# The first half's residual of a two-layer convolution kernel, moved to ScalarE and an accumulating DMA

## The chip, the core and the metric

The kernel runs on one core of a Trainium2 chip. Its time is the device time of one launch in microseconds (us); a smaller time is better. All numbers below are of this one core. TensorE is called PE in the rows, VectorE DVE, ScalarE ACT, GpSimd POOL, SyncE SP.

## What is computed

The input `x` has 16 images of 128 channels and 64 x 64 pixels. Two residual layers follow each other, each on a group norm of its input (32 groups of 4 channels):

```
def adc(y):                                   # step 2^-8, clip at +-16
    return clip(round(y * 0.01 / step) * step, -16, 16)
# layer 0: quantised input, a cubic term, a 3x3 convolution with three weight planes
v    = dac(_gn(x) * input_factor)             # 8 bits, scaled to 0.6
fv   = patches(v) + 0.1 * patches(v) ** 3
outs = [einsum('bctfyx,ocyx->btfo', fv, g[i]) for i in range(3)]
mem  = adc(outs[2]) + 4 * adc(outs[0]) + 2 * adc(outs[1]) + adc(outs[2])
x    = x + mem * output_factor + bias
# layer 1: q, k, v projections of _gn(x), 64 channels each
out  = q * (eB @ (exp(k) * v)) / (eB @ exp(k))
x    = x + Wm @ out
```

The three `adc` results of layer 0 are whole numbers and are kept as int16; their sum times `fin` (twice the step times the output factor) plus the bias is the layer's output, and it is added to the image.

## The kernel before

One image is a tile `xr[m]` of 128 channels x 4096 pixels in f32; four such tiles form a ring. The work on an image is written as a *phase* of 36 *slots* (0 to 35). Every engine runs its own program, written out slot by slot by `phase`, so the order of each engine is fixed by the tables at the head of the file (`BIAS = (17, 32)`: in slots 17 and 32) and by the order of the `if` lines in `phase`. Engines meet only in semaphores. An instruction that waits holds up all that is behind it on its engine.

In phase p TensorE convolves image p: two halves of 2048 pixels, in each the three planes, which makes six *steps* n = 0 to 5 of six slots each. In every slot TensorE does one product of 9 matmuls (lines 504 to 506) of 512 columns. The rows are transformed beforehand (`transform` on VectorE, `rows_high` on ScalarE, `rows_low` on GpSimd). The products of a step go to a bank pair `A` and to the low pair `B`. `copy_m2` (line 836, ScalarE) copies `B` out, in slot place 2 of each step; `mix_middle` (lines 1192 to 1204, VectorE) forms the four output rows from `A` and the copy; `adc_round` (line 844, ScalarE) turns two of them into int16 in `uall`, and frees the bank pair. It runs two steps late: the rounding of n = 4 stands in slot 0 of the next phase, and TensorE's product in slot 2 of that phase (`middle`, `j == 1`) waits for it. Between these products stands layer 1 of the two images before: in eight slots per phase TensorE does projections (line 586), sums (line 614) and mixes (line 636). Before the projections of slot 32 it waits for `copy_m2` of step 5; before the sums for line 1280 of VectorE.

The end of layer 0 on one half h: `combine_planes` and `first_residual` (VectorE) clip and add the three planes in int16 (lines 1210 to 1225), and line 1228 adds `fin` times the sum to the image. Before that `add_bias` (line 856, ScalarE) has added the bias in place. Then `stats_x1` (line 809, ScalarE, with a one-element shift, line 800, ahead of an image's first) reads the finished pixels in four quarters of 1024, two passes each, for the group norm of layer 1. The first half's quarters stand in slots 26 and 31, the second half's in slots 8 and 9 of the next phase.

Layer 1's output goes back in the way that the change borrows: ScalarE writes it to a buffer `y2` in `shared` (line 901) and GpSimd issues a DMA that adds it to the image (line 1528, 512 KB each, four per image). SyncE loads the image after next (line 404) and stores results (line 414).

A loop of four phases is repeated; the first two phases, phases 2 to 5 and the last three are written out apart.

Of the kernel before, what the change touches and what calls it, by code (L numbers as in the profile page):

```python
# [20 lines left out]
ALU = mybir.AluOpType  # L21
ACT = mybir.ActivationFunctionType
# [44 lines left out]
COMBINE = (20, 0)  # L67
DOUBLE = (17, 35)
RESIDUAL = (23, 8)
BIAS = (17, 32)  # L70
X1_STATS = (26, 31, 8, 9)
X1_SPREAD = 12
X1_GROUP = 15
LOW = (28, 33, 8, 11)
# [28 lines left out]
def conv_layers_kernel(nc, x, g_pos, g_neg, bias, in_factor, out_factor, Wq, Wk, Wv, Bm, Wm, out):  # L103
# [6 lines left out]
    with ctx:  # L110
        def sb(name, shape, dt=F32):
            return ctx.enter_context(nc.sbuf_tensor(name, shape, dt))

        def sem(name):
            return ctx.enter_context(nc.semaphore(name))
# [8 lines left out]
        T = sb("T", [P, 2, 3, H // 4, 2, W], F16)  # L124

        shared = sb("shared", [P, NP * 4 * 3 * P + 4 * 3 * P])
        y2 = [shared[:, k * PX:(k + 1) * PX] for k in range(2)]
        pieces = [shared[:, 4 * PX + k * HALF:4 * PX + (k + 1) * HALF] for k in range(4)]
        t32 = sb("t32", [P, 3, TILES, 2, W])
# [141 lines left out]
        summed = sem("summed")  # L271
        combined = sem("combined")
        biased = sem("biased")
        first_done = sem("first_done")
        tail_part = sem("tail_part")
        tail_stats = sem("tail_stats")
# [443 lines left out]
        def _(act):  # L720
# [94 lines left out]
                channel_stats(0, xr[m], image, q, before)  # L815

            def stats_x1(image, m, q, before):
                act.wait_ge(first_done, nth(image, HALVES, q // 2))
                channel_stats(1, xr[m], image, q, before)

            def last_stats(m):
# [16 lines left out]
            def adc_round(p, n, first):  # L838
                h, i = divmod(n, NP)
                act.wait_ge(conv_ready, nth(p, STEPS, n))  # L840
                if not first or h:

                    act.wait_ge(first_done if i else summed, nth(p, HALVES, h - 1))
                nc.scalar.copy(u[i].rearrange("p (t k c) -> p k t c", k=4, c=W)[:, 0:4:3],  # L844
                               A[n % 2][:, :, :].rearrange("p e (t w) -> p e t w", w=W)).then_inc(rounded, 1)

# [4 lines left out]
                act.wait_ge(inner_made, nth(p, STEPS, NP * h))  # L851
                nc.scalar.activation(u[0], u[0], ACT.Identity, scale=2.0).then_inc(doubled, 1)

            def add_bias(p, m, h):
                xh = xr[m][:, h * HPX:(h + 1) * HPX]
                nc.scalar.activation(xh, xh, ACT.Identity, bias=bcol[:, :]).then_inc(biased, 1)

            def z_high(image, m, k, w):
# [62 lines left out]
            def phase(p, m, images):  # L921
                prev2, prev, cur, nxt = images
                first = not prev
                before, two_before, after = (m + 3) % RING, (m + 2) % RING, (m + 1) % RING
                for slot in range(SLOTS):
                    n, place = divmod(slot, 6)
                    if first and slot == 0:
                        level(0, 0, 3)
                    if first and slot == 1:
                        cubic(0, 3)  # L930
                    if place == 0 and n < 2 and prev and cur:
                        adc_round(p - 1, STEPS - 2 + n, False)
                    if not cur and slot in (0, 2):
                        adc_round(p - 1, STEPS - 2 + slot // 2, False)
                    if place == 0 and n >= 2 and cur:
                        adc_round(p, n - 2, first)
                    if place == 2 and cur:
                        copy_m2(p, n, first)
                    second_layer(p, m, slot, images)
                    if first and slot in (3, 9):  # L940
                        high_weights(1 + slot // 9)
                    if first and slot == 14:
                        small_weights()
                    if nxt and slot in X_STATS:
                        q = X_STATS.index(slot)
                        stats_x(p + 1, after, q, (0, p + 1, q - 1) if q else (1, p - 1, 1) if prev else (0, p, 3))
                    if not cur and slot == X1_STATS[2]:
                        last_stats(before)
                    if prev and cur and slot in X1_STATS[2:]:
                        q = X1_STATS.index(slot)  # L950
                        stats_x1(p - 1, before, q,
                                 (1, p - 1, 2) if q == 3 else (0, p + 1, 3) if nxt else (1, p - 1, 1))
                    if cur and slot in X1_STATS[:2]:
                        q = X1_STATS.index(slot)
                        stats_x1(p, m, q, (1, p, 0) if q else (1, p - 1, 3) if prev else (0, p + 1, 3))
                    if cur and slot in DOUBLE:
                        double(p, DOUBLE.index(slot))
                    if cur and slot in BIAS:
                        add_bias(p, m, BIAS.index(slot))
                    if cur and slot in HIGH[2:]:  # L960
                        rows_high(p, m % 2, HIGH.index(slot))
                    if nxt and slot in LEVEL:
                        level(p + 1, after, LEVEL.index(slot))
                    if nxt and slot in SQUARE:
                        cubic(p + 1, SQUARE.index(slot))
                    if nxt and slot in HIGH[:2]:
                        rows_high(p + 1, 1 - m % 2, HIGH.index(slot))
                if not cur and prev:
                    z_high(p - 1, before, 0, 0)
                    z_high(p - 1, before, 1, 1)  # L970
                    for k in range(NG):
                        exponent(p - 1, k, k)
                        if k < NG - 2:
                            z_high(p - 1, before, k + 2, k + 2)
                        if k:
                            guess(p - 1, k - 1, k - 1)
                    guess(p - 1, NG - 1, NG - 1)
# [22 lines left out]
        def _(dve):  # L1000
# [161 lines left out]
            def mix_middle(p, n, images):  # L1162
# [22 lines left out]
                    dve.wait_ge(t_ready, nth(p, NG, 1))  # L1185
                if i == 0 and (prev or h):
                    dve.wait_ge(summed, nth(p, HALVES, h - 1))
                if i == 1 and (prev or h):
                    dve.wait_ge(first_done, nth(p, HALVES, h - 1))

                near, far = bank[:, 0, :], bank[:, 1, :]
                nc.vector.tensor_tensor(minus, near, m2[:, 0, :], ALU.subtract)  # L1192
# [21 lines left out]
                dve.wait_ge(clipped, nth(p, 2 * HALVES, 2 * h + 1))  # L1214
                nc.vector.tensor_tensor(u[1], u[0], u[1], ALU.add).then_inc(summed, 1)

            def first_residual(p, m, h):

                xh = xr[m][:, h * HPX:(h + 1) * HPX]
                dve.wait_ge(rounded, nth(p, STEPS, NP * h + 2))  # L1220
                dve.wait_ge(inner_made, nth(p, STEPS, NP * h + 2))
                nc.vector.tensor_scalar(u[2], u[2], CLIP, -CLIP, ALU.min, ALU.max).then_inc(clipped_last, 1)
                dve.wait_ge(summed, nth(p, HALVES, h))
                dve.wait_ge(clipped_last, nth(p, HALVES, h))
                nc.vector.tensor_tensor(u[1], u[1], u[2], ALU.add).then_inc(combined, 1)  # L1225
                dve.wait_ge(combined, nth(p, HALVES, h))
                dve.wait_ge(biased, nth(p, HALVES, h))
                nc.vector.scalar_tensor_tensor(out=xh, in0=u[1], scalar=fin[:, :], in1=xh, op0=ALU.mult, op1=ALU.add  # L1228
                                               ).then_inc(first_done, 1)

            def last_residual(m):
# [3 lines left out]
                dve.wait_ge(rounded, nth(p, STEPS, NP * h + 2))  # L1235
                dve.wait_ge(inner_made, nth(p, STEPS, NP * h + 2))
                dve.wait_ge(summed, nth(p, HALVES, h))
                dve.wait_ge(biased, nth(p, HALVES, h))
                for c in range(2):
                    cols = slice(c * PX, (c + 1) * PX)  # L1240
                    xh = xr[m][:, (2 + c) * PX:(3 + c) * PX]
# [15 lines left out]
            def last_sums(m):  # L1257


                count = 1.0 * PX  # L1260
                dve.wait_ge(first_done, HALVES * B)
                for h in range(2):
                    at = 3 * PX + h * HALF
                    nc.vector.bn_stats(hst[:, h, :], xr[m][:, at:at + HALF]).then_inc(tail_stats, 1)
# [80 lines left out]
            def phase(p, m, images):  # L1345
# [3 lines left out]
                for slot in range(SLOTS):  # L1349
# [17 lines left out]
                        g = TRANSFORM.index(slot)  # L1367
                        transform(p, g, mixed(p, slot))
                    if prev and cur and slot == RESIDUAL[1]:
                        first_residual(p - 1, before, 1)  # L1370
                    if not cur and slot == 3:
                        last_residual(before)
                        last_sums(before)
# [8 lines left out]
                    if cur and slot == COMBINE[0]:  # L1382
                        combine_planes(p, 0)
                    if cur and slot == RESIDUAL[0]:
                        first_residual(p, m, 0)
                    if nxt and slot in QUANTISE:
                        quantise(p + 1, QUANTISE.index(slot))
                    if nxt and slot in CUBIC:
# [45 lines left out]
        def _(pool):  # L1434
# [90 lines left out]
            def add_mix(image, m, k):  # L1525
# [2 lines left out]
                nc.gpsimd.dma_start(xr[m][:, k * PX:(k + 1) * PX], y2[k % 2], accum_op=ALU.add  # L1528
                                    ).then_inc(y_added[k % 2], 16)

            def second_layer(p, m, slot, images):

                at = second("Z_POOL", p, slot, images)
                if at:
                    z_rest(at[0], at[2])
                at = second("ADD_POOL", p, slot, images)
                if at:
                    add_mix(at[0], (m + at[1]) % RING, at[2])

            def phase(p, m, images):  # L1540
                prev2, prev, cur, nxt = images
                before, two_before = (m + 3) % RING, (m + 2) % RING
                for slot in range(SLOTS):
                    second_layer(p, m, slot, images)
                    if cur and slot in LOW[2:]:
                        rows_low(p, m % 2, LOW.index(slot))
                    if nxt and slot in LOW[:2]:
                        rows_low(p + 1, 1 - m % 2, LOW.index(slot))
                    if nxt and slot == X_MOMENTS:
                        scale_x(p + 1)  # L1550
                    if prev and slot == X1_MOMENTS:
                        scale_z(p - 1)
# [37 lines left out]
```

## Time and profile before

| | |
|---|---|
| time, median of 3 runs | 1532.73 us (1531.08 to 1533.22) |
| profiled execution, span from first to last instruction | 1530.4 us |
| TensorE busy | 1446.2 us, 95% |
| VectorE busy | 1402.8 us, 92% |
| ScalarE busy | 1191.8 us, 78% |
| GpSimd busy | 521.5 us, 34% |
| mean granted TensorE clock | 0.984 |
| DMA | 103.91 MB, 68 GB/s mean |

Of the profiled execution only the span is given; the median of the runs is 2.3 us above it. The middle of the program is periodic: between two neighbouring images the same instructions come 89.2 us later, so one period can be read for all. A matmul's record lasts about 0.38 us, but the next starts 0.216 us after it; the busy time of TensorE counts overlaps once. A row of the timeline gives start, duration, engine, line, operation, output and input, and in brackets how long the engine was idle before and who ended it.

### The profile page before, as it was taken

To read this page: it belongs to the slowest core of one execution; us is meant where nothing else is said; L and a number is where in the kernel's file an instruction comes from. 1 tells how busy PE (TensorE), PEld (TensorE's weight loads), DVE (VectorE), ACT (ScalarE), POOL (GpSimd) and SP (SyncE) were. 2 spreads that over 40 slices of the span, in tenths; PEclk is the share of its full clock that TensorE was granted. 3 is DMA by queue.
4 is the path that set the end of the run, shared out by engine and by line. 5 is a ranking of instruction groups with operands and counts; after the bars stand their busy time and mean duration, and the time that the engine had idled before them with its cause. 6 is when DMAs were issued, how large, how long until landed. Compare 5 with 4: busy or idle time off the path is not lost.

```text
span 1530.4 us, 24432 instructions
## 1 busy us (share of the span) xinstructions
PE 1446.2 (95%) x8560; PEld 645.4 (42%) x8560; DVE 1402.8 (92%) x2185; ACT 1191.8 (78%) x1561; POOL 521.5 (34%) x503
## 2 busy tenths in 40 slices
PE   2799999999999999999999999999999999999975
PEld 2444444444444444444444444444444444444422
DVE  7879999999999999999999998999999999999766
ACT  4557788788878878887887888788788878876563
POOL 3111334234333433333343343334333333433312
PEclk9799999999999999999999999999999999999997
DMA  5011012223122222312222231232223122212222
GB/s 208 1 56 42 14 28 56 83 56 111 42 64 89 56 83 56 111 42 69 84 56 84 56 111 43 57 96 56 83 56 110 39 62 95 56 28 56 69 70 83
DMA packets 29180, 103.91 MB, mean 68 GB/s; under 512 B 4032, under 2 KB 4224, under 8 KB 29056
## 3 DMA queue, kind: packets, MB, share of 16 engines
q1 hardware_dynamic: 20416, 70.86, 12.4%
q0 software_dynamic: 8640, 31.46, 10.9%
q8 instruction: 70, 1.15, 0.3%
q14 instruction: 54, 0.44, 0.1%
HBM read 37.29 MB, written 33.55 MB: 46 GB/s over the span
## 4 chain that ended last, share of the span: by engine, by line
DVE 50%; PE 28%; issue 14%; ACT 5%; POOL 1%; DVEq 1%; DMA 0%; SPq 0%; ACTq 0%; POOLq 0%
PE A L504 5%; PE A L505 5%; PE A L506 5%; DVE duo L1132 3%; DVE uall L1225 3%; DVE A L1195 3%; DVE A L1204 3%; DVE uall L1198 3%; DVE duo L1192 3%; DVE uall L1200 2%; DVE duo L1193 2%; DVE A L1196 2%; DVE f L1109 2%; PE B L504 2%; PE B L505 2%
## 5 line engine op out<-in xcount | busy, mean ns | idle before, releaser
L504 PE MATMUL A<-T,WH 128*128 128x504 f16 (+1 forms) x1152 | 438.4, 381 | 0.0
L506 PE MATMUL A<-T,WL 128*128 128x504 f16 (+1 forms) x1152 | 437.3, 380 | 0.0
L505 PE MATMUL A<-T,WH 128*128 128x504 f16 (+1 forms) x1152 | 437.3, 380 | 0.0
L1521 POOL TENSOR_TENSOR T<-t,T 128x512 f16<-128x512 f32 x189 | 254.9, 1374 | 424.8 <-ACT T L766 424.8
L1495 POOL TENSOR_TENSOR zl<-z,zh 128x512 f16<-128x512 f32 x120 | 158.5, 1337 | 434.3 <-ACT zh L877 434.3
L809 ACT ACTIVATE junk<-xr,shift 128x1024 f16<-128x1024 f32 x244 | 280.1, 1148 | 5.5
L504 PE MATMUL B<-T,WH 128*128 128x504 f16 (+1 forms) x576 | 221.0, 384 | 19.1 <-DVE T L1158 11.5
L505 PE MATMUL B<-T,WH 128*128 128x504 f16 (+1 forms) x576 | 220.9, 383 | 0.0
L506 PE MATMUL B<-T,WL 128*128 128x504 f16 (+1 forms) x576 | 220.7, 383 | 0.0
L504 PEld LDWEIGHTS A<-T,WH 128*128 128x128 f16 x1152 | 115.4, 100 | 164.3 <-issue 46.4
L506 PEld LDWEIGHTS A<-T,WL 128*128 128x128 f16 x1152 | 112.7, 98 | 136.2
L505 PEld LDWEIGHTS A<-T,WH 128*128 128x128 f16 x1152 | 112.7, 98 | 117.9
L746 ACT ACTIVATE q<-xr,bi,sc 128x1024 int16<-128x1024 f32 x64 | 79.2, 1240 | 62.6 <-DVE f L1109 40.9
L844 ACT CAST uall<-A 128x1024 int16<-128x1024 f32 x96 | 96.2, 1002 | 32.3 <-PE A L506 32.0
L836 ACT COPY m<-B 128x1024 f32<-128x1024 f32 x96 | 96.0, 1000 | 30.0 <-PE B L506 30.0
L766 ACT CAST T<-t 128x512 f16<-128x512 f32 x192 | 105.7, 614 | 9.9 <-DVE t L1148 9.6
L504 PEld LDWEIGHTS B<-T,WH 128*128 128x128 f16 x576 | 56.6, 98 | 100.7 <-issue 21.8
L881 ACT ACTIVATE shared<-L 128x512 f32<-128x512 f32 x61 | 36.2, 593 | 66.6 <-PE L L586 66.6
L1228 DVE SCALAR_TENSOR_TENSOR xr<-uall,fin,xr 128x2048 f32<-128x2048 int16 x31 | 85.9, 2770 | 1.1
L506 PEld LDWEIGHTS B<-T,WL 128*128 128x128 f16 x576 | 56.8, 99 | 69.7 <-issue 2.8
L901 ACT ACTIVATE shared<-B 128x1024 f32<-128x1024 f32 x60 | 61.3, 1022 | 31.9 <-PE B L636 31.9
L1528 POOL DMA_DIRECT2D xr<-shared x60 | 53.3, 889 | 92.4 <-ACT shared L901 92.4
(186 smaller groups left out, 2563.7 us busy)
## 6 DMA issues: line engine op xcount, KB each, us to landing
xr<-in_x_dram SPq DMA_DIRECT2D x64, 512.0 KB, 5.8
out_dram<-xr SPq DMA_DIRECT2D x64, 512.0 KB, 2.7
xr<-shared POOLq DMA_DIRECT2D x60, 512.0 KB, 4.5
xr<-in_L_conv_g_pos_dram SPq DMA_DIRECT2D x3, 576.0 KB, 9.8
xr<-in_L_conv_g_neg_dram SPq DMA_DIRECT2D x3, 576.0 KB, 11.6
xr<-in_L_conv_Wm_dram SPq DMA_DIRECT2D x2, 32.0 KB, 9.6
xr<-in_L_conv_Wq_dram SPq DMA_DIRECT2D x1, 32.0 KB, 11.6
xr<-in_L_conv_Wk_dram SPq DMA_DIRECT2D x1, 32.0 KB, 11.4
```

What stands on the lines that cost most here:

```text
L504: nc.tensor.matmul(to, wh, th, start=fresh and y == 1, stop=False, skip_group_check=True)
L505: nc.tensor.matmul(to, wh, tl, start=False, stop=False, skip_group_check=True)
L506: done = nc.tensor.matmul(to, wl, th, start=False, stop=y == 2, skip_group_check=True)
L746: nc.scalar.activation(q16[b][:, :], xr[m][:, q * PX:(q + 1) * PX], ACT.Identity, bias=bi1[:, :], scale=sc1[:, :]).then_inc(leveled, 1)
L766: nc.scalar.copy(T[:, 0, pair, g * TILES:(g + 1) * TILES, :, :], t32[:, pair]).then_inc(th_ready, 1)
L809: nc.scalar.activation(junk[:, :], src[:, q * PX:(q + 1) * PX], func, bias=shift[which][:, :], accum_out=moments[which][:, k, q:q + 1]).th ...
L836: nc.scalar.copy(m2[:, :, :], low_pair[:, :, :]).then_inc(m2_copied, 1)
L844: nc.scalar.copy(u[i].rearrange("p (t k c) -> p k t c", k=4, c=W)[:, 0:4:3], A[n % 2][:, :, :].rearrange("p e (t w) -> p e t w", w=W)).the ...
L901: nc.scalar.activation(y2[k % 2].rearrange("p (r c n) -> p c r n", r=2, n=QUART), low_pair[:, :, :].rearrange("p c (r n) -> p c r n", r=2) ...
L1228: nc.vector.scalar_tensor_tensor(out=xh, in0=u[1], scalar=fin[:, :], in1=xh, op0=ALU.mult, op1=ALU.add).then_inc(first_done, 1)
L1495: nc.gpsimd.tensor_tensor(zl[0][:, cols], z32[:, cols], zh[0][:, cols], ALU.subtract).then_inc(zl_ready, 1)
L1521: last = nc.gpsimd.tensor_tensor(low, t32[:, pair, :, :, :].rearrange("p t e w -> p (t e w)"), high, ALU.subtract)
```

## The change

For the first half of an image (h = 0) line 1228 and its `add_bias` go. In their place a new `first_output` on ScalarE computes `fin * sum + bias` from the int16 sum into `y1`, 2048 columns of `shared` that are free by then, and a new `first_add` on GpSimd issues one DMA of 1 MB that adds `y1` to the first half of the image. The statistics of the first two quarters wait for that DMA and stand in slots 31 and 34 in place of 26 and 31. The second half is as before.

```
-BIAS = (17, 32)
-X1_STATS = (26, 31, 8, 9)
+OUTPUT = 26
+OUTPUT_ADD = 27
+BIAS = 32
+X1_STATS = (31, 34, 8, 9)
...
+        y1 = shared[:, 2 * PX:4 * PX]
...
             def stats_x1(image, m, q, before):
-                act.wait_ge(first_done, nth(image, HALVES, q // 2))
+                if q < 2:
+                    act.wait_ge(first_added, nth(image, 16, 15))
+                else:
+                    act.wait_ge(first_done, nth(image, 1, 0))
                 channel_stats(1, xr[m], image, q, before)
...
+            def first_output(p):
+                act.wait_ge(combined, nth(p, HALVES, 0))
+                if isinstance(p, int) and p == 0:
+                    act.wait_ge(small_done, 1)
+                    act.wait_ge(w_turned, 9)
+                else:
+                    act.wait_ge(first_added, nth(p, 16, 15, 1))
+                nc.scalar.activation(y1, u[1], ACT.Identity, bias=bcol[:, :], scale=fin[:, :]).then_inc(y1_made, 1)
...
-            def add_bias(p, m, h):
-                xh = xr[m][:, h * HPX:(h + 1) * HPX]
+            def add_bias(p, m):
+                xh = xr[m][:, HPX:2 * HPX]
...
-            def first_residual(p, m, h):
+            def sum_planes(p, h):
...
                 nc.vector.tensor_tensor(u[1], u[1], u[2], ALU.add).then_inc(combined, 1)
-                dve.wait_ge(combined, nth(p, HALVES, h))
-                dve.wait_ge(biased, nth(p, HALVES, h))
+
+            def first_residual(p, m):
+                xh = xr[m][:, HPX:2 * HPX]
+                dve.wait_ge(combined, nth(p, HALVES, 1))
+                dve.wait_ge(biased, nth(p, 1, 0))
                 nc.vector.scalar_tensor_tensor(out=xh, in0=u[1], scalar=fin[:, :], in1=xh, op0=ALU.mult, op1=ALU.add
                                                ).then_inc(first_done, 1)
...
                     if cur and slot == RESIDUAL[0]:
-                        first_residual(p, m, 0)
+                        sum_planes(p, 0)
...
+            def first_add(p, m):
+                waits_apart(pool, (y1_made, nth(p, 1, 0)))
+                nc.gpsimd.dma_start(xr[m][:, 0:HPX], y1, accum_op=ALU.add).then_inc(first_added, 16)
```

The waits that guard `u[1]` and `u[2]` (in `adc_round` and `mix_middle`) are put on the new semaphores: plane 1 of the second half waits for `y1_made`, plane 2 for `combined`.

ScalarE in slots 26 to 32 of a phase in the middle, before (`m` is the copy of the low pair, `xr,shift` the statistics, `uall<-A` the rounding, `T<-t` the rows, `f<-q` the square of the quantised input):

```order
L836 COPY m<-B 128x1024
L800 ACTIVATE shift<-xr 128x1
L809 ACTIVATE junk,moments<-xr,shift 128x1024 x2
L756 ACTIVATE f<-q 128x1024
L844 CAST uall<-A 128x2x8x64
L766 CAST T<-t 128x512 x3
L809 ACTIVATE junk,moments<-xr,shift 128x1024 x2
L836 COPY m<-B 128x1024
```

The same slots now:

```order
L844 COPY m<-B 128x1024
L878 ACTIVATE shared<-uall,bcol,fin 128x2048
L761 ACTIVATE f<-q 128x1024
L859 CAST uall<-A 128x2x8x64
L771 CAST T<-t 128x512 x3
L805 ACTIVATE shift<-xr 128x1
L814 ACTIVATE junk,moments<-xr,shift 128x1024 x2
L844 COPY m<-B 128x1024
```

The new output pass has taken the place of the first quarter's statistics, and these, with their shift, now stand behind the rows and right ahead of the copy of step 5.

ScalarE from slot 32 to slot 0 of the next phase, before (`shared<-L` and `shared<-B` are exponents, logarithm and query copy of layer 1, `z` and `zh` its normalised input, `uall<-uall` the doubling):

```order
L856 ACTIVATE xr<-xr,bcol 128x2048
L766 CAST T<-t 128x512 x3
L887 ACTIVATE shared<-L 128x512
L889 ACTIVATE shared<-shared 128x512
L893 COPY shared<-B 128x512
L872 ACTIVATE z<-xr,bi,rs 128x1024
L877 CAST zh<-z 128x1024
L852 ACTIVATE uall<-uall 128x2048
L844 CAST uall<-A 128x2x8x64
```

The same stretch now:

```order
L882 ACTIVATE xr<-xr,bcol 128x2048
L771 CAST T<-t 128x512 x3
L913 ACTIVATE shared<-L 128x512
L915 ACTIVATE shared<-shared 128x512
L919 COPY shared<-B 128x512
L814 ACTIVATE junk,moments<-xr,shift 128x1024 x2
L898 ACTIVATE z<-xr,bi,rs 128x1024
L903 CAST zh<-z 128x1024
L867 ACTIVATE uall<-uall 128x2048
L859 CAST uall<-A 128x2x8x64
```

The second quarter's statistics have come in ahead of `z`, and so ahead of the rounding of step 4, the last row.

GpSimd from slot 18 to slot 35, before (`zl` is the low part of layer 1's input, `T` the low part of the rows, six pieces in two groups):

```order
L1495 TENSOR_TENSOR zl<-z,zh 128x512 x2
L1528 DMA xr<-shared 128x1024
L1495 TENSOR_TENSOR zl<-z,zh 128x512 x2
L1521 TENSOR_TENSOR T<-t,T 128x512 x6
L1495 TENSOR_TENSOR zl<-z,zh 128x512 x2
L1528 DMA xr<-shared 128x1024
```

The same slots now:

```order
L1529 TENSOR_TENSOR zl<-z,zh 128x512 x2
L1562 DMA xr<-shared 128x1024
L1529 TENSOR_TENSOR zl<-z,zh 128x512 x2
L1569 DMA xr<-shared 128x2048
L1555 TENSOR_TENSOR T<-t,T 128x512 x6
L1529 TENSOR_TENSOR zl<-z,zh 128x512 x2
L1562 DMA xr<-shared 128x1024
```

The new DMA, twice as wide as the others, is issued ahead of the low parts of the rows; nothing else has moved.

## Rows read from the trace of the kernel before

**Rows 1.** Page, part 1: busy us, share of the span, instructions.
```profile
PE 1446.2 (95%) x8560; PEld 645.4 (42%) x8560; DVE 1402.8 (92%) x2185; ACT 1191.8 (78%) x1561; POOL 521.5 (34%) x503
```
**Rows 2.** Stretch 700 to 800: length, busy PE, PEld, DVE, ACT, POOL, clock, DMA share, GB/s.
```profile
700.00:800.00 100.00, 99.28 (x583) 44.11 (x582) 95.17 (x158) 84.00 (x108) 38.99 (x42) 1.00 0.26 72
```
**Rows 3.** Waits of PE, whole run: us in total, times, longest.
```profile
PE L L614 <- DVE shared L1280: 8.3, 15, 0.9
...
PE L L586 <- ACT m L836: 4.2, 12, 0.7
```
**Rows 4.** Page, part 4: the chain that ended last, by engine.
```profile
DVE 50%; PE 28%; issue 14%; ACT 5%; POOL 1%; DVEq 1%; DMA 0%; SPq 0%; ACTq 0%; POOLq 0%
```
**Rows 5.** Timeline of PE, slot 32 to slot 2 of the next phase.
```profile
741.64 1.05 PE L586 MATMUL L<-zh,wqkv 128*64 128x512 f16 x8 [0.21 <-ACT m L836]
...
747.47 1.09 PE L614 MATMUL L<-shared,eb 64*64 64x256 f32 x16 [0.51 <-DVE shared L1280]
...
756.29 0.38 PE L504 MATMUL A<-T,WH 128*128 128x512 f16 x1
```
**Rows 6.** Timeline of ACT, slot 24 to slot 0 of the next phase.
```profile
725.54 1.24 ACT L746 ACTIVATE q<-xr,bi,sc 128x1024 int16<-128x1024 f32 x1 [0.63 <-DVE f L1109]
...
729.85 1.01 ACT L836 COPY m<-B 128x1024 f32<-128x1024 f32 x1
730.75 0.20 ACT L800 ACTIVATE shift<-xr 128x1 f32<-128x1 f32 x1
730.99 1.15 ACT L809 ACTIVATE junk<-xr,shift 128x1024 f16<-128x1024 f32 x1
...
735.63 1.01 ACT L844 CAST uall<-A 128x1024 int16<-128x1024 f32 x1 [1.18 <-PE A L506]
...
738.18 1.15 ACT L809 ACTIVATE junk<-xr,shift 128x1024 f16<-128x1024 f32 x1
...
740.59 0.99 ACT L836 COPY m<-B 128x1024 f32<-128x1024 f32 x1
...
745.22 1.99 ACT L856 ACTIVATE xr<-xr,bcol 128x2048 f32<-128x2048 f32 x1
...
750.29 1.24 ACT L872 ACTIVATE z<-xr,bi,rs 128x1024 f32<-128x1024 f32 x1
...
752.52 1.91 ACT L852 ACTIVATE uall<-uall 128x2048 int16<-128x2048 int16 x1
754.33 0.99 ACT L844 CAST uall<-A 128x1024 int16<-128x1024 f32 x1
```
**Rows 7.** Line 1228 in the whole run: min, median, max in ns.
```profile
L1228 DVE SCALAR_TENSOR_TENSOR xr<-uall,fin,xr x31: 2351/2352/3308, 114.7 to 1444.9; 128x2048 f32<-128x2048 int16 x31
```
**Rows 8.** Timeline of DVE: the sum of the first half's planes, and line 1280.
```profile
726.21 1.23 DVE L1225 TENSOR_TENSOR uall<-uall 128x2048 int16<-128x2048 int16 x1
...
746.64 0.69 DVE L1280 SCALAR_TENSOR_TENSOR shared<-L,shared 128x512 f32<-128x512 f32 x1
```
**Rows 9.** Timeline: an ACT pass into the buffer, and the DMA issue that waits for it.
```profile
718.38 1.01 ACT L901 ACTIVATE shared<-B 128x1024 f32<-128x1024 f32 x1
```
**Rows 10.** The same place on POOL.
```profile
719.94 0.96 POOL L1528 DMA_DIRECT2D xr<-shared  x1 [4.64 <-ACT shared L901]
```
**Rows 11.** Line 1528 in the whole run: from issue to landing.
```profile
DMA to landing us min/median/max: 4.5/4.5/6.1
```
**Rows 12.** Page, part 3, the queue of line 1528: packets, MB, share of 16 engines.
```profile
q0 software_dynamic: 8640, 31.46, 10.9%
```
**Rows 13.** Timeline of PE, a pause in the first phases.
```profile
135.81 0.38 PE L504 MATMUL B<-T,WH 128*128 128x512 f16 x1 [2.30 <-issue]
```
**Rows 14.** Stretch 135 to 140, columns as in rows 2.
```profile
135.00:140.00 5.00, 4.19 (x13) 1.68 (x14) 4.90 (x8) 3.33 (x6) 0.71 (x1) 0.70 0.10 16
```
**Rows 15.** Timeline of ACT and PE in the last image's phases.
```profile
1471.35 1.24 ACT L872 ACTIVATE z<-xr,bi,rs 128x1024 f32<-128x1024 f32 x1
...
1474.48 1.41 PE L586 MATMUL L<-zh,wqkv 128*64 128x512 f16 x8 [2.79 <-DVE shared L1296]
```

More of the change, by code:

```diff
@@ L273, in conv_layers_kernel @@
         biased = sem("biased")
+        y1_made = sem("y1_made")
+        first_added = sem("first_added")
         first_done = sem("first_done")
@@ L841, in adc_round @@
                 if not first or h:
-                    act.wait_ge(first_done if i else summed, nth(p, HALVES, h - 1))
+                    if i == 0:
+                        act.wait_ge(summed, nth(p, HALVES, h - 1))
+                    elif i == 2:
+                        act.wait_ge(combined, nth(p, HALVES, h - 1))
+                    elif h:
+                        act.wait_ge(y1_made, nth(p, 1, 0))
+                    else:
+                        act.wait_ge(first_done, nth(p, 1, 0, 1))
                 nc.scalar.copy(u[i].rearrange("p (t k c) -> p k t c", k=4, c=W)[:, 0:4:3],
@@ L852, in double @@
                 nc.scalar.activation(u[0], u[0], ACT.Identity, scale=2.0).then_inc(doubled, 1)
-            def add_bias(p, m, h):
-                xh = xr[m][:, h * HPX:(h + 1) * HPX]
+            def first_output(p):
[3 more added lines that the diff above has]
+                    act.wait_ge(w_turned, 9)
+                else:
+                    act.wait_ge(first_added, nth(p, 16, 15, 1))
+                nc.scalar.activation(y1, u[1], ACT.Identity, bias=bcol[:, :], scale=fin[:, :]).then_inc(y1_made, 1)
+            def add_bias(p, m):
+                xh = xr[m][:, HPX:2 * HPX]
                 nc.scalar.activation(xh, xh, ACT.Identity, bias=bcol[:, :]).then_inc(biased, 1)
@@ L957, in phase @@
                         double(p, DOUBLE.index(slot))
-                    if cur and slot in BIAS:
-                        add_bias(p, m, BIAS.index(slot))
+                    if cur and slot == OUTPUT:
+                        first_output(p)
+                    if cur and slot == BIAS:
+                        add_bias(p, m)
                     if cur and slot in HIGH[2:]:
@@ L1187, in mix_middle @@
                     dve.wait_ge(summed, nth(p, HALVES, h - 1))
-                if i == 1 and (prev or h):
-                    dve.wait_ge(first_done, nth(p, HALVES, h - 1))
+                if i == 1 and h:
+                    dve.wait_ge(y1_made, nth(p, 1, 0))
+                elif i == 1 and prev:
+                    dve.wait_ge(first_done, nth(p, 1, 0, 1))
                 near, far = bank[:, 0, :], bank[:, 1, :]
@@ L1215, in combine_planes @@
                 nc.vector.tensor_tensor(u[1], u[0], u[1], ALU.add).then_inc(summed, 1)
-            def first_residual(p, m, h):
-                xh = xr[m][:, h * HPX:(h + 1) * HPX]
+            def sum_planes(p, h):
                 dve.wait_ge(rounded, nth(p, STEPS, NP * h + 2))
@@ L1237, in last_residual @@
                 dve.wait_ge(summed, nth(p, HALVES, h))
-                dve.wait_ge(biased, nth(p, HALVES, h))
+                dve.wait_ge(biased, nth(p, 1, 0))
                 for c in range(2):
@@ L1260, in last_sums @@
                 count = 1.0 * PX
-                dve.wait_ge(first_done, HALVES * B)
+                dve.wait_ge(first_done, B)
                 for h in range(2):
@@ L1369, in phase @@
                     if prev and cur and slot == RESIDUAL[1]:
-                        first_residual(p - 1, before, 1)
+                        sum_planes(p - 1, 1)
+                        first_residual(p - 1, before)
                     if not cur and slot == 3:
@@ L1546, in phase @@
                         rows_low(p, m % 2, LOW.index(slot))
+                    if cur and slot == OUTPUT_ADD:
+                        first_add(p, m)
                     if nxt and slot in LOW[:2]:
```

## The prediction, made before the changed kernel was run

> **What bounds the kernel now.** The page's chain of waits puts half of the span on VectorE [rows 4], and VectorE is busy 92% [rows 1]. That reads as if each VectorE instruction taken away were time won. So the next view is the busy time in a stretch of the middle: from 700 to 800 us TensorE is busy 99.28 of 100, VectorE 95.17, ScalarE 84.00 [rows 2]. TensorE is the wall; the chain only runs over VectorE because the two are close. The list of waits then says what is left to win: TensorE waits for VectorE's line 1280 before the sums, 8.3 us in the whole run, and for ScalarE's copy of the low pair before the projections, 4.2 us [rows 3], 12.5 us together. Both stand in one place of the period, slots 32 and 33: 0.21 us at 741.64 and 0.51 at 747.47 [rows 5].
>
> Last the timeline of ScalarE around that place, since the change puts its work there. ScalarE waits for TensorE at 735.63; from then on it is behind. Its copy of step 5 starts at 740.59 and is what TensorE waits for at 741.64; the rounding of step 4 runs from 754.33 to 755.3 [rows 6], and TensorE's product that needs it starts at 756.29 without a wait [rows 5]. So there is 0.96 us of room at the second place and none at the first.
>
> **What is removed.** Line 1228 on the first half, 16 of its instructions. The fastest of them takes 2.35 us [rows 7], so at least 38 us of VectorE's busy time go. The whole of it lies beside TensorE's work. It can pay no more than TensorE's waits for VectorE, 8.3 us, since line 1280 at 746.64 [rows 8] comes about 2 us sooner. I take that 0.5 us per image as won, inside the sum below. `add_bias` on the first half (1.99 us, as in rows 6) goes from slot 17, where ScalarE next waits for GpSimd: worth nothing.
>
> **What is added on ScalarE.** The output pass reads 2048 int16 per partition. Nearest rows: the doubling, int16, 1.91 us; the bias pass, 1.99; and a pass with scale and bias both from memory takes 1.24 for 1024 columns [rows 6] against 1.01 for one without [rows 9], so 0.2 more. I take 2.1 us; bounds 1.9 and 2.5 (twice 1.24). It stands behind the copy of step 4, which ends near 730.8 [rows 6]. The sum it needs ends at 727.44 [rows 8], so it does not wait. The level pass at 725.54 waited 0.63 us for VectorE [rows 6], and a less burdened VectorE gives most of that back, so I start the output pass at 730.2 and end it at 732.3. ScalarE had idle time there, 1.18 us before 735.63 plus what the first quarter's statistics (730.75 to 733.4) leave: covered.
>
> **The DMA.** GpSimd's issue starts 0.55 us after the pass (718.38 + 1.01 = 719.39 to 719.94) [rows 9, 10]. From issue to landing the 512 KB DMAs of this kind take 4.5 us [rows 11]. Their queue's packets take 10.9% of the span [rows 12], 166.8 us over 60 DMAs, 2.78 us each. So 1.7 us are fixed, and 1 MB should take 1.7 + 5.6 = 7.3 us. Landing: 732.3 + 0.55 + 7.3 = 740.15. The bounds are 4.5 us (size costs nothing) and 9.0 (twice all of it), so 737.35 to 742.2 with the passes' bounds.
>
> The Trainium skill, "DMA: Bandwidth & Descriptors", section "Anatomy of one DMA — SWDGE (gpsimd) path", fits a DMA issued by GpSimd with about 2.0 us plus bytes at 436 GB/s. By that 512 KB would take 3.2 us and the new one 4.4 (an estimate from the page). This trace does not agree for the accumulating kind: it shows 4.5 at 512 KB [rows 11].
>
> **First wait, slot 31.** Behind the rows, ScalarE is free at 738.18 [rows 6] and now waits for the landing until 740.15, 2.0 us. Then come the shift, 0.24 (730.75 to 730.99), and the quarter's two passes, 2.41 (738.18 to 740.59). The copy of step 5 starts at 742.8 in place of 740.59: 2.2 us late. Queued behind it are the projections of slot 32, on TensorE itself, so TensorE stands 2.4 us there in place of 0.2. At the sums the old 0.5 us goes. Net after that point: 1.7.
>
> **Second wait, slot 0.** ScalarE's exponent, output copy and bias pass follow TensorE's projections and are late by the same 2.2 us. Then, ahead of `z` (750.29), the second quarter's 2.41 us are new. The rounding of step 4 ends at 755.33 + 2.2 + 2.4 = 759.9, and TensorE's product of slot 2 starts then, not at 756.29. That is 3.6 us late per image, whatever was lost at the first wait: 2.2 + 2.4 less the room of 0.96. Behind it ScalarE has idle places and VectorE is no longer full, so both are level with TensorE again by the middle of the next phase. The loss comes back once per image.
>
> In the rows, it adds to 14 images, the phases 1 to 14: 14 x 3.6 = 50. In phase 0 layer 1 is missing and ScalarE has room: I put 1 there, a choice. In the last phases ScalarE's `z` at 1471.35 would come 2.4 + 0.5 us later, and TensorE's projections at 1474.48 hang on it [rows 15]: 3. Sum 54, on a span of 1530.4: 1584.4. The median of the runs lies 2.3 above the profiled span, so **1587 us**.
>
> Bounds: if the DMA lands before ScalarE asks (4.5 us), only 0.24 + 2.41 - 0.96 = 1.7 per image stays, 24 + 3, which gives 1560. If it takes 9.0 us, landing at 742.2, the loss is 4.3 + 2.4 - 0.96 = 5.7 per image, 80 + 5, which gives 1618.
>
> **The rivals.**
> 1. *The DMA is hidden, only the order costs.* As the lower bound: 1560 (1553 to 1569). For it: the fixed part may cover more than the 1.7 us. Against it: 2.78 of the present DMA's 4.5 us are packets [rows 11, 12]. The Trainium skill's fit named above would give this case, 4.4 us against the 5.3 that are free between the issue at 732.85 and 738.18.
> 2. *The clock falls on top.* After a pause of 2.30 us in front of 135.81 [rows 13] the granted clock is 0.70 over the next 5 us, and TensorE's work there is 13 matmuls against 5 / 0.216 = 23 at full pace [rows 14]. The level granted in part of that stretch is the lower one, 1.2 GHz. My first wait is 2.4 us long, as much as that one. If each brings 1.5 us (half of a 3 us stretch at the low level), 14 x 1.5 = 21: 1608 (1600 to 1625). Against it: part of that is spent before ScalarE's late rounding anyway.
> 3. *Faster, since VectorE is the bound.* The place is slots 32 and 33: with VectorE 2.35 us ahead, TensorE's waits there fall away, at most 12.5 us over the run, which gives 1520 (1518 to 1529). It decides if ScalarE's new work at 738 to 755 costs less than the 0.96 us of room plus its idle time, so if the landing comes before 738 and the 2.4 us of the second quarter find gaps. For it: rows 4. Against it: ScalarE has no bracket of idle time in front of 738.18, 740.59, 750.29, 752.52 or 754.33 [rows 6]; it is full there.
> 4. *No change*: the gains of 3 and the losses meet, or the wait sits where nobody is late: 1533.
>
> **How the numbers follow.** The forecast (landing after 738.18, both waits) gets 0.60, with 1570 to 1600 as its own range. Rival 1 gets 0.13, rival 2 0.14, rival 3 0.08, rival 4 0.05. The range reaches from rival 1 to the upper bound and into rival 2: 1556 to 1618. About 0.2% (3 us) is what a measurement of this kernel can tell from no change. Slower: forecast and rivals 1 and 2, 0.87; within it: 0.05; faster: 0.08.
>
> **What the profile after would show.** Right: line 814's first pass behind the rows is preceded by about 2 us of ScalarE idle, ended by the DMA of line 1569; that DMA takes near 7.3 us from issue to landing; the projections of slot 32 show TensorE idle about 2.4 us, released by the copy of the low pair; the product of slot 2 shows about 2 us, released by the rounding; the sums of slot 33 show no wait for VectorE; the period is 92.8 us in place of 89.2. VectorE's busy time falls by about 40 us. Wrong in size: landing at 4.5 us or at 9. Wrong in kind: the period is 89 or less, which would mean that ScalarE's work of slots 30 to 36 has more room than the timeline shows; or the granted clock is below 1.00 in the middle, which is rival 2.

## The result, and the profile after

The changed kernel takes 1608.45 us (1602.46 to 1610.01, 4 runs) against 1531.9 before: a ratio of 1.049, 95% interval 1.047 to 1.051. It is slower, as forecast, and inside the range; the point of 1587 us was 21 us too low.

The page of the kernel after, busy time and the chain that ended last:

```profile
PE 1466.0 (91%) x8560; PEld 648.1 (40%) x8560; DVE 1400.4 (87%) x2169; ACT 1191.1 (74%) x1561; POOL 547.0 (34%) x519
...
DVE 30%; PE 24%; ACT 19%; issue 16%; DMA 7%; POOL 3%; DVEq 0%; ACTq 0%; SPq 0%; POOLq 0%
```

Against [rows 1] VectorE's and ScalarE's busy times are nearly the same in a longer span, TensorE's is 20 us longer over the same 8560 instructions, and GpSimd's is 25.5 us longer over 16 more. Against [rows 4] ScalarE's share of the chain has risen from 5% to 19% and the DMA's from 0% to 7%. TensorE's waits say where:

```profile
PE L L591 <- ACT m L844: 43.1, 15, 3.6
PE A L509 <- ACT uall L859: 24.5, 14, 1.9
```

The first is the wait for the copy of step 5, 4.2 us in [rows 3]; the second, for the rounding of step 4, was not there. Both come once per image. Periods are counted from TensorE's group statistics in slot 14, which stand at 828.4 here and at 701.5 in the kernel before. ScalarE in the period from 828.4 on, the answer to [rows 6]:

```profile
852.56 1.24 ACT L751 ACTIVATE q<-xr,bi,sc 128x1024 int16<-128x1024 f32 x1 [0.70 <-DVE f L1137]
...
857.77 2.10 ACT L878 ACTIVATE shared<-uall,bcol,fin 128x2048 f32<-128x2048 int16 x1
...
862.58 1.01 ACT L859 CAST uall<-A 128x1024 int16<-128x1024 f32 x1 [1.76 <-PE A L511]
863.49 1.66 ACT L771 CAST T<-t 128x512 f16<-128x512 f32 x3
867.46 0.20 ACT L805 ACTIVATE shift<-xr 128x1 f32<-128x1 f32 x1 [2.31 <-DMA xr<-shared]
...
870.11 0.99 ACT L844 COPY m<-B 128x1024 f32<-128x1024 f32 x1
...
879.80 1.15 ACT L814 ACTIVATE junk<-xr,shift 128x1024 f16<-128x1024 f32 x1
...
882.22 1.23 ACT L898 ACTIVATE z<-xr,bi,rs 128x1024 f32<-128x1024 f32 x1
...
886.25 0.99 ACT L859 CAST uall<-A 128x1024 int16<-128x1024 f32 x1
```

The output pass runs from 857.77 to 859.87. ScalarE is done with the rows at 865.15 and stands still until the DMA has landed, 2.31 us. From 867.46 it has no pause of its own until 870.11. The second quarter (879.80) stands ahead of `z`, and the rounding ends at 887.24. The DMA itself, line 1569, all 16:

```profile
DMA to landing us min/median/max: 6.9/7.0/8.3
```

TensorE in the same period, the answer to [rows 5]: 2.78 us at the projections, no wait at the sums, 1.90 at slot 2.

```profile
871.16 1.05 PE L591 MATMUL L<-zh,wqkv 128*64 128x512 f16 x8 [2.78 <-ACT m L844]
...
876.41 1.10 PE L619 MATMUL L<-shared,eb 64*64 64x256 f32 x16
...
887.29 0.39 PE L509 MATMUL A<-T,WH 128*128 128x512 f16 x1 [1.90 <-ACT uall L859]
```

Two neighbouring periods of the kernel after, columns as in [rows 2]:

```profile
734.20:828.40 94.20, 90.10 (x529) 39.15 (x529) 85.38 (x133) 74.62 (x99) 34.31 (x33) 0.98 0.30 79
828.40:921.60 93.20, 88.52 (x529) 38.71 (x529) 85.43 (x133) 74.66 (x99) 34.36 (x33) 1.00 0.30 80
```

The undisturbed period is 93.2 us, 4.0 more than the 89.2 of before. The other has 1.0 on top and a mean clock of 0.98. Its cause stands behind the first wait; TensorE's row, and the windows of the stretch:

```profile
776.96 1.05 PE L591 MATMUL L<-zh,wqkv 128*64 128x512 f16 x8 [2.77 <-ACT m L844]
```
```profile
776.00:778.20 2.20, 1.25 (x12) 0.60 (x12) 2.20 (x5) 0.90 (x2) 0.00 (x0) 1.00 0.00 0
778.20:781.60 3.40, 3.40 (x23) 1.23 (x20) 2.65 (x5) 1.57 (x3) 0.00 (x0) 0.50 0.00 0
```

After a pause of 2.77 us the granted clock is 0.50, the lower level of 1.2 GHz, for 3.4 us. Such a fall came in 11 of the 14 periods, and in none of the 14 of before.

So the 77.5 us that the span grew by (1530.4 to 1607.9) are: 14 x 4.05 = 57 of waits at full clock; 15 put down to the clock, as a difference (the 14 periods sum to 1323.5 us; 14 x 93.2, and the 3.8 us by which the 14 before exceed 14 x 89.14, make 1308.6; 11 falls of 3.4 us at half the clock could cost at most 19); 6 after the last period (118.0 against 111.9 us); less 0.3 in the stretch ahead of the first period.

### The profile page after: what moved, and what is told of

The parts are those of the page before. It is cut to its first block, busy times and chain, and to the rows that moved or that the text cites. A ratio compares the mean times of both kernels' runs of the same rounds, so it can differ in the third digit from the quotient of the medians.

```text
span 1607.9 us, 24442 instructions
## 1 busy us (share of the span) xinstructions
PE 1466.0 (91%) x8560; PEld 648.1 (40%) x8560; DVE 1400.4 (87%) x2169; ACT 1191.1 (74%) x1561; POOL 547.0 (34%) x519
## 4 chain that ended last, share of the span: by engine, by line
DVE 30%; PE 24%; ACT 19%; issue 16%; DMA 7%; POOL 3%; DVEq 0%; ACTq 0%; SPq 0%; POOLq 0%
DMA xr<-shared 7%; PE A L509 4%; PE A L510 4%; PE A L511 4%; PE L L591 4%; ACT z L898 3%; PE B L641 3%; ACT junk L814 3%; POOL zl L1529 3%; DVE f L1137 2%; DVE A L1225 2%; DVE A L1234 2%; DVE uall L1228 2%; DVE duo L1222 2%; ACT uall L859 2%
## 5 line engine op out<-in xcount | busy, mean ns | idle before, releaser
L1555 POOL TENSOR_TENSOR T<-t,T 128x512 f16<-128x512 f32 x189 | 244.8, 1320 | 431.3 <-ACT T L771 431.3
L1529 POOL TENSOR_TENSOR zl<-z,zh 128x512 f16<-128x512 f32 x120 | 176.7, 1489 | 454.8 <-ACT zh L903 454.8
L591 PE MATMUL L<-zh,wqkv 128*64 128x512 f16 x492 | 71.3, 415 | 51.7 <-ACT m L844 43.1
L1160 DVE TENSOR_TENSOR duo<-f 128x1024 f32<-128x1024 f32 x64 | 91.6, 1432 | 7.6 <-POOL T L1555 3.7
L1562 POOL DMA_DIRECT2D xr<-shared x60 | 58.7, 978 | 94.8 <-ACT shared L927 89.5
L1222 DVE TENSOR_TENSOR duo<-A,m 128x512 f32<-128x512 f32 x96 | 65.6, 683 | 26.8 <-issue 17.7
```

What stands on the lines that cost most here:

```text
L591: last = nc.tensor.matmul(out, lhsT, src, start=m == 0, stop=m == 2, skip_group_check=True)
L1160: nc.vector.tensor_tensor(flat, f[:, at + 2:at + 2 + ROWS, :], f[:, at:at + ROWS, :], ALU.subtract).then_inc(delta_made, 1)
L1529: nc.gpsimd.tensor_tensor(zl[0][:, cols], z32[:, cols], zh[0][:, cols], ALU.subtract).then_inc(zl_ready, 1)
L1555: last = nc.gpsimd.tensor_tensor(low, t32[:, pair, :, :, :].rearrange("p t e w -> p (t e w)"), high, ALU.subtract)
```

## The experiments

Each is timed against the kernel before, run again on the same chip; its medians there were 1531.9, 1532.2 and 1532.0 us, so the runs can be compared with each other too.

**Order alone.** Kernel before, without the new DMA and the output pass:
```
-X1_STATS = (26, 31, 8, 9)
+X1_STATS = (31, 34, 8, 9)
```


> The kernel before with one table changed: the first half's statistics in slots 31 and 34 in place of 26 and 31. VectorE's residual, the bias pass and all DMAs stay. Theory (ScalarE is full from slot 30 to slot 0 of the next phase, with 0.96 us of room): the shift (0.24) and one quarter (2.41) more stand ahead of the rounding of step 4, so TensorE's product of slot 2 waits 1.7 us per image; 14 images and about 3 at the end give 1532 + 27 = 1559 us, and TensorE's wait at the projections of slot 32 grows by only 0.24. Rival (the loss is the DMA's alone, its wait and its traffic): no change, 1532 us.

Measured: 1558.77 us, ratio 1.017 (1.016 to 1.019). TensorE's waits:
```profile
PE A L504 <- ACT uall L844: 20.5, 14, 1.6
...
PE L L586 <- ACT m L836: 8.1, 15, 0.7
```
The wait at slot 2 is there without the new DMA. 27 us of the loss are the place of the statistics.

**The DMA's landing.** Kernel after:
```
-        first_added = sem("first_added")
+        first_added = [sem("first_added0"), sem("first_added1")]
...
-                    act.wait_ge(first_added, nth(image, 16, 15))
+                    act.wait_ge(first_added[q], nth(image, 16, 15))
...
-                nc.gpsimd.dma_start(xr[m][:, 0:HPX], y1, accum_op=ALU.add).then_inc(first_added, 16)
+                for c in range(2):
+                    cols = slice(c * PX, (c + 1) * PX)
+                    nc.gpsimd.dma_start(xr[m][:, cols], y1[:, cols], accum_op=ALU.add).then_inc(first_added[c], 16)
```


> The changed kernel with its 1 MB DMA issued as two of 512 KB, each with its own semaphore, so that a quarter's statistics wait only for their own part. Theory (the first loss is ScalarE's wait for the landing): the first lands 4.5 us after its issue, when ScalarE is just free; ScalarE's 2.3 us of waiting and most of TensorE's 2.8 us at slot 32 go, the granted clock no longer falls, and the 1.7 to 2.1 us at slot 2 stay: 1560 to 1566 us. Rival (the traffic of the added 1 MB, or GpSimd's issue of it, is what costs): two issues cost at least as much as one, 1600 us or more.

Measured: 1556.53 us, ratio 1.016 (1.014 to 1.017), the same as with the order alone and some 4 us under the theory's range.
```profile
PE A L509 <- ACT uall L859: 26.3, 14, 2.1
...
PE L L591 <- ACT m L844: 8.6, 15, 1.6
```
The wait for the copy fell from 43.1 to 8.6 us, and the clock's falls from 11 of 14 periods to 1. The 1 MB still moves. So 52 us, the falls of the clock included, hung on when the first quarter lands.

**The traffic.** Kernel before, with one more DMA per image that nobody waits for:
```
...
+                nc.gpsimd.dma_start(shared[:, 3 * PX:4 * PX], shared[:, 2 * PX:3 * PX], accum_op=ALU.add
+                                    ).then_inc(extra, 16)
...
```


> The kernel before with one more accumulating DMA of 512 KB per image, inside a free part of the shared buffer, issued by GpSimd in slot 27 as in the changed kernel, which nobody but the next one of its kind waits for. Theory (the traffic and its issue cost nothing by themselves): 1532 us within 0.2%. Rival (the added traffic slows engines or the other DMAs): half of the unexplained part, 1540 us or more.

Measured: 1532.75 us, ratio 0.9997 (0.999 to 1.001). An added DMA of 512 KB and its issue cost nothing that can be measured here. That is half of the change's bytes.

**VectorE's part alone.** Kernel before:
```
-                nc.vector.scalar_tensor_tensor(out=xh, in0=u[1], scalar=fin[:, :], in1=xh, op0=ALU.mult, op1=ALU.add
-                                               ).then_inc(first_done, 1)
+                n = HPX if h else 1
+                nc.vector.scalar_tensor_tensor(out=xh[:, 0:n], in0=u[1][:, 0:n], scalar=fin[:, :], in1=xh[:, 0:n],
+                                               op0=ALU.mult, op1=ALU.add).then_inc(first_done, 1)
```


> The kernel before with VectorE's residual of an image's first half over 1 of its 2048 columns (the other 2047 are left without the first layer's output), so that some 36 us of VectorE's work are gone and nothing is put in their place. Theory (TensorE bounds, VectorE is only close): TensorE's wait for line 1280 at slot 33, 0.5 us per image, goes and nothing else: 1525 us, down to 1520. Rival (VectorE bounds, as the chain of waits reads): 1532 - 36 = 1496 us.

Measured: 1526.08 us, ratio 0.996 (0.994 to 0.998). This is all that freeing VectorE brings by itself. By the theory TensorE's wait for it at the sums would be gone; it fell from 8.3 to 4.8 us:
```profile
PE L L614 <- DVE shared L1281: 4.8, 14, 0.6
```
VectorE's busy time fell by 10.4 us only, though the shortened instruction gave up 34. In 14 of its 64 places the next `duo<-f` takes 2.17 us in place of 1.22, each time beside GpSimd's `zl`:
```profile
817.15 2.45 POOL L1496 TENSOR_TENSOR zl<-z,zh 128x512 f16<-128x512 f32 x2 [9.19 <-ACT zh L877]
```
```profile
818.51 2.17 DVE L1132 TENSOR_TENSOR duo<-f 128x1024 f32<-128x1024 f32 x1
```

**The bias pass in slot 17.** Kernel after, `BIAS = 32` to `BIAS = 17`:

> The changed kernel with the second half's bias pass in slot 17, where ScalarE waits for GpSimd, in place of slot 32. Theory (slot 2's wait is ScalarE being full between slots 30 and 0): 1.99 us leave that stretch, the 2.0 us wait of slot 2 goes, the 2.8 us at slot 32 and the falls of the clock stay: 1608 - 14 x 2.0 = 1580 us. Rival (the second wait only follows from the first, as everything behind a late DMA): 1605 us or more, since the first is untouched.

Measured: 1597.04 us, ratio 1.043 (1.041 to 1.045). Neither number came. The wait at slot 2 went from 2.06 us (the 1.90 of the row and what the pipeline hides) to 1.46. ScalarE shows why:
```profile
871.78 0.60 ACT L913 ACTIVATE shared<-L 128x512 f32<-128x512 f32 x1 [1.20 <-PE L L619]
```
Of the 1.99 us taken out, 1.20 are now idle time in front of the logarithm, which waits for TensorE's sums. What counts at slot 2 is the row of work behind the sums, and the bias pass stands ahead of it. The clock fell in 5 periods only, though the pauses ahead were as long as before (2.7 to 4.1 us, against 2.7 to 3.7). The two profiled executions are 15.8 us apart: 14 x 0.57 = 8 us are the undisturbed period, 92.6 in place of 93.2, some 6 are the clock, by the same difference as above, and 2 lie ahead of the first period and behind the last. Why the clock fell less often stays open.

**Both edits.** Two DMAs and the bias pass in slot 17:

> The changed kernel with both edits: the DMA issued as two, and the second half's bias pass in slot 17. Theory (the second wait is the length of ScalarE's row of work from TensorE's sums of slot 33 to the rounding of step 4, and the bias pass stands ahead of that row, where 1.2 of its 1.99 us are idle time once it is gone): from the two-DMA kernel's 1557 only 0.6 us per image go, 1548 us, and 1.4 us of waiting stay at slot 2. Rival (only ScalarE's total in slots 30 to 36 counts): all 1.99 us go, 1557 - 28 = 1529 us.

Measured: 1550.24 us, ratio 1.012 (1.010 to 1.013), near the 1548 of that reading. The undisturbed period fell by 0.6 to 0.7 us, to 90.2.

**The bias pass moved in the kernel before**, `BIAS = (17, 17)`:

> The kernel before with both bias passes in slot 17. Theory: nobody waits for the bias pass of slot 32 and TensorE does not wait at slot 2, so 1532 us within 0.2%; the 1.99 us in front of slot 17's level pass are partly idle time of ScalarE, partly ahead of it (1.48 us idle before, so the level pass may come 0.5 us later): up to 1536. Rival (the bias pass is a load on the row to slot 0 there too): 1525 us or less.

Measured: 1534.59 us, ratio 1.0016 (1.0006 to 1.0025). No gain, and 2.5 us lost, which is clear of noise. That is inside the 1532 to 1536 of the theory, and far from the rival's 1525.

**A better order.** The two-DMA kernel with the second quarter behind the rounding, and one quarter of a later image's input statistics in ScalarE's idle place at slot 28:
```
+X1_STATS = (31, 0, 8, 9)
+X_EARLY = 28
...
+                    if prev and slot == X1_STATS[1]:
+                        stats_x1(p - 1, before, 1, (1, p - 1, 0))
+                    if nxt and slot == X_EARLY and not (isinstance(p, int) and p + 2 >= B):
+                        stats_x(p + 2, two_before, 0, (1, p - 1, 3) if prev else (0, p + 1, 3))
...
```


> The two-DMA kernel with the second quarter's statistics moved from slot 34 to slot 0 of the next phase, behind the rounding, and the input statistics of the first quarter of the image after next moved from slot 0 to slot 28 of the phase before, where ScalarE waits 1.76 us for TensorE. Theory: the wait at slot 2 goes (2.06 us per image); the rows of slot 30 and the copy of step 5 come 0.9 us later, so the wait at slot 32 is 1.4 us in place of 0.5: 1557 - 14 x 1.1 = 1541 us. Rival (the loss is in the DMA and the number of passes, not in their places): 1555 us or more.

Measured: 1534.34 us, ratio 1.001 (1.000 to 1.002), better than I expected: the period is 89.4 us, and all that is left of the waits is at the copy, 1.1 to 1.2 us an image:
```profile
PE L L592 <- ACT m L845: 16.6, 15, 1.4
```
The wait at slot 2 is gone, 2.06 us. The one at slot 32 grew by 0.5 us (8.6 us in the run to 16.6) where I had put 0.9. So 1.5 us per image came in place of 1.1.

**Behind the copy.** On top, the first quarter stands in slot 32 between the copy of step 5 and the exponent, where ScalarE waits for TensorE:
```
+X1_STATS = (32, 0, 8, 9)
...
                         copy_m2(p, n, first)
+                    if cur and slot == X1_STATS[0]:
+                        early = nxt and not (isinstance(p, int) and p + 2 >= B)
+                        stats_x1(p, m, 0, (0, p + 2, 0) if early else (1, p - 1, 3))
                     second_layer(p, m, slot, images)
...
```


> As the kernel with both moves, but with the bias pass left in slot 32. Theory: the row of work from the exponent to the rounding of step 4 is 1.99 us longer than there, of which 1.2 fill an idle place; TensorE waits about 0.5 us at slot 2: 1526 us. Rival (the bias pass costs nothing where it is): the same time as with it in slot 17.

Measured: 1522.31 us (1522.09 to 1525.94), ratio 0.994 (0.993 to 0.995). The period is 88.7 us, and the waits for the copy and the rounding are gone, also the 0.5 us that the theory had left at slot 2; TensorE waits for VectorE at the sums again, 0.4 to 0.5 us an image:
```profile
PE L L620 <- DVE shared L1321: 6.6, 15, 0.7
```

With the bias pass in slot 17 as well:

> The rearranged two-DMA kernel with two more moves: the first quarter's statistics stand behind the copy of step 5 in slot 32, where ScalarE waits 1.58 us for TensorE's projections, and the second half's bias pass in slot 17. Theory: the copy is ready when TensorE asks (its 1.15 us wait goes), the exponent comes 1.1 us later, which VectorE and the sums of slot 33 can bear, and the rounding of step 4 is in time: a period of 88.3 us in place of 89.2, 1520 us (1517 to 1524). Rival (the move only puts the wait elsewhere, at the sums or at slot 2): 1530 us or more.

Measured: 1526.46 us (1522.62 to 1526.73), ratio 0.996 (0.994 to 0.997). Its forecast, 1520 us from a period of 88.3, was missed: part of the wait has moved to the sums, as its rival had it, though not to 1530. The undisturbed periods are those of the kernel with the pass in slot 32, to 0.01 us, so the bias pass costs nothing at either place: the rival of that kernel held. The runs of both kernels spread from 1522 to 1527 us. In the two profiled executions, 1523.6 and 1520.8 us long, the difference lies ahead of the first period (1.9 us) and behind the last (1.5), and not in them (0.6 the other way).

With the change's single DMA of 1 MB in that last kernel:

> As the kernel with both moves, but with the change's own single DMA of 1 MB. Theory: it lands 39.0 us after the group statistics of the phase, the statistics now ask for it at about 40, so nobody waits and the time is that of the two-DMA kernel within 0.2%. Rival (two smaller DMAs are needed): 1.5 us or more of waiting return per image, 1540 us.

Measured: 1527.28 us, ratio 0.996 (0.995 to 0.998). One DMA of 1 MB is as good as two once it is asked for late.

**A like move without the change.** Kernel before, the second quarter behind the copy in slot 32:
```
-X1_STATS = (26, 31, 8, 9)
+X1_STATS = (26, 32, 8, 9)
```


> The kernel before with only this edit: the second quarter's statistics in slot 32 behind the copy of step 5, in place of slot 31 ahead of it. Theory: the 0.3 us wait for the copy goes, but VectorE's 0.57 us at the sums of slot 33 stays, since the residual is still VectorE's: 1528 us. Rival (all of what the rearranged kernels win is ScalarE's order, and none comes from freeing VectorE): 1520 us, as the changed kernel with the same moves.

Measured: 1531.8 us, ratio 1.0001 (0.999 to 1.001). The wait for the copy went, and VectorE's grew by the same:
```profile
PE L L614 <- DVE shared L1281: 12.2, 15, 1.0
```
It was 8.3 in [rows 3]. The 1528 of the theory did not come either: what ScalarE gave up, TensorE now waits for VectorE. The one-column kernel has VectorE freed and gains 0.4%, this one a changed order and gains nothing; the kernel with both gains 0.6% (0.5 to 0.7) and is the fastest of all. That it needs both is shown for this one move of the order. The whole order of the best kernel (first quarter behind the copy, second in slot 0, input statistics in slot 28) was not tried on the kernel before.

## Why the prediction was right, and where its size was off

- **What bounds.** TensorE does, and VectorE's removed instruction is worth 0.4% and not the 2.4% of its duration: shown by the one-column kernel. So the mechanism of the forecast was right: work moved to where ScalarE had no room, and the loss came at the two waits that were named. Reading the chain of waits alone would have given the wrong sign.
- **VectorE's busy time** was to fall by 40 us. It fell by 2.4. Line 1228 lost 37.5 us, but what stood behind it moved on top of GpSimd's low parts of `z`. Kernel after, VectorE and GpSimd:
```profile
857.37 2.18 DVE L1160 TENSOR_TENSOR duo<-f 128x1024 f32<-128x1024 f32 x1
```
```profile
857.11 3.45 POOL L1529 TENSOR_TENSOR zl<-z,zh 128x512 f16<-128x512 f32 x2 [9.17 <-ACT zh L903]
...
884.67 2.27 POOL L1529 TENSOR_TENSOR zl<-z,zh 128x512 f16<-128x512 f32 x2 [3.90 <-ACT zh L903]
```
  The `duo<-f` instructions, 122 us before, take 149 after, line by line 13.4 us more in each of two groups; GpSimd's `zl`, 158.5, take 176.7, while its `T` sums became 10 us shorter (254.9 to 244.8). This expectation was wrong. The one-column kernel shows that the new DMA is not the cause: it has neither that DMA nor the output pass, and the same instruction takes 2.17 us there, again beside `zl`. A sign of it stood in [rows 7]: line 1228 takes 2.35 us at the median and 3.31 at most, and the 14 long ones (3.13 to 3.31) are those of the second half that lie wholly beside GpSimd's `T` sums. TensorE's waits for VectorE's line 1280 went all the same.
- **The output pass**: 2.10 us against 2.1 taken. That it starts 0.5 us earlier was wrong: the level pass ahead of it still waits 0.70 us for VectorE. The removed line 1228 stood behind the work for which that pass waits [rows 6, 8], so nothing was freed ahead of it.
- **The DMA**: 7.0 us from issue to landing against 7.3, so scaling the packets of the 512 KB ones over a fixed part came out within 0.3 us. The Trainium skill's fit ("DMA: Bandwidth & Descriptors", "Anatomy of one DMA — SWDGE (gpsimd) path"), by which 1 MB would take an estimated 4.4 us, does not hold for this accumulating DMA, at 7.0.
- **The two waits.** ScalarE stood 2.31 us (2.0 forecast), TensorE 2.8 and 2.1 us (2.4 and 1.9 forecast, the latter being 3.6 less 1.7), and the sums' wait went. The period is 93.2 against the 92.8 forecast; 57 us in place of 50. The 0.4 us come with the output pass. Counted from the start of the period it begins 0.6 us later than forecast (29.3 against 28.7), the issue follows 0.64 us behind its end and not 0.55, since GpSimd is at `zl` until then, and the DMA is 0.3 us shorter.
- **The clock** was rival 2, given 0.14 and priced at 21 us. It came on top of the forecast and cost 15. This is the term of the sum that was missing: with it the forecast's own working gives 1602. The measured 1608 lies outside the forecast's own 1570 to 1600 and inside rival 2's range. That it equals rival 2's number is luck: there the clock is 6 us too high, and the waits and the end together 10 too low. A pause of 2.30 us with a fall behind it stood in [rows 13, 14], and the forecast itself made a pause of 2.4 us per image; the two should have been one case.
- **The end** cost 6 us and not 3. Phase 0 cost nothing, where 1 had been put.
- **Rivals 1 and 3**: a hidden DMA leaves the loss of the order, 1560; the order alone measured 1559 and the two-DMA kernel 1557. Faster needed ScalarE's work to find room at slots 30 to 36, and it did not there; placed elsewhere it did.

## What to carry to other kernels

Before giving an engine more work, look for the deadline in each place of its row: here ScalarE was busy 78%, but from slot 30 to slot 0 every instruction stood between two waits of TensorE, with 0.96 us to spare. A DMA in place of an instruction has a landing time that someone must be able to wait for. Put the wait where that engine is idle anyway. Asked for there, one DMA of 1 MB cost no more than two of 512 KB (1527 and 1526 us), where at the first place it cost 52 us more. And when work is removed from an engine that is not the bound, count what that can release, at most 12.5 us of waits here, of which 5.8 came, not the work's duration.

## What the runs showed of the hardware that was not expected

Taking a VectorE instruction out made others longer. In the kernel after, the two `duo<-f` instructions gained 13.4 us each and GpSimd's `zl` 18, while line 1228 gave 37.5 and GpSimd's `T` sums 10. The 14 long ones of each `duo<-f` (2.18 and 1.64 us) all overlap with a `zl`; the 50 others do not, and take 1.21 to 1.23 and 0.68 to 0.69. In the one-column kernel, where `zl` ends before the second `duo<-f` begins, only the first one is long, and in the kernel before none is. So the longer times go with the overlap of the two engines and not with the DMA. In the rows at 857, the pair of `zl` takes 3.45 us beside `duo<-f`, 1.2 more than the 2.27 of the pair at 884.67 in the same period, and 1.2 is what the first `duo<-f` takes alone.

The granted clock fell behind 11 of 14 pauses of 2.7 to 3.7 us in the kernel after, for 3.4 us each time, and behind 5 of 14 in the kernel with the bias pass moved. In the kernel after, pauses of 2.74 us had a fall behind them and one of 2.79 us had none. The pause's length alone does not decide it; what else does is open.
